# Where a step of the edge stage does its share of the next group's binning

## The reference

```python
xn = _layernorm(x, axis=-1)
x = x + _L0_gnn_ref(xn, edge_weight, src, dst) + _L0_mix_ref(xn[None], ...)[0]
x = x + _L0_ffn_ref(_layernorm(x, axis=-1)[None], ...)[0]
...
def _L0_gnn_ref(x, values, row, col):     # row = src, col = dst
    msgs = values[:, None] * x[col]
    return jax.ops.segment_sum(msgs, row, num_segments=N_NODES)
```

## Time and profile before

| | |
|---|---|
| median of 3 runs | 2460.25 us (2447.17 to 2464.95) |
| the profiled execution | 2457.84 us, span 2455.5 us, mean granted TensorE clock 0.938 |
| TensorE matmul busy | 2100.7 us (86%) |
| TensorE weight loads busy | 1796.0 us (73%) |
| VectorE / ScalarE / GpSimd busy | 1567.8 (64%) / 1074.1 (44%) / 1503.6 (61%) |
| gathers L1087 | 1029, mean 1186 ns |
| edge stage | from 339.2 us to about 1947 us of the span |

### The profile page before, as it was taken

One profiled execution on the slowest core, in us unless ns is written; L12 is line 12 of the kernel. 1 busy time (PEld: TensorE's weight loads), 2 busy tenths in 40 slices (PEclk: granted clock), 3 DMA queues, 4 the chain that ended last, 5 costly groups with the idle time before them and its releaser, 6 DMA issues. The chain is left out here.

```text
span 2455.5 us, 39205 instructions
## 1 busy us (share of the span) xinstructions
PE 2100.7 (86%) x11850; PEld 1796.0 (73%) x11851; DVE 1567.8 (64%) x2845; ACT 1074.1 (44%) x3171; POOL 1503.6 (61%) x1293
## 2 busy tenths in 40 slices
PE   4678668999899889989998999899999883888880
PEld 2356557888788778878887888788888783666660
DVE  6787558866786788578758875877444459233326
ACT  2331025556455545655555555555666420222220
POOL 1000268877777777688778877867777530676760
PEclk8898889999999999999999999999999856999995
DMA  5422372223222322233232223222333420566658
GB/s 194 161 81 71 109 234 77 85 86 95 78 82 86 93 76 83 85 89 86 85 88 85 84 87 91 78 85 84 91 101 101 120 99 0 167 186 181 186 163 313
DMA packets 157053, 271.50 MB, mean 111 GB/s; under 512 B 27730, under 2 KB 104513, under 8 KB 156770
## 3 DMA queue, kind: packets, MB, share of 16 engines
q0 software_dynamic: 59584, 161.78, 22.0%
q1 hardware_dynamic: 84534, 91.92, 12.1%
q10 hardware_dynamic: 12780, 15.84, 1.8%
HBM read 224.64 MB, written 45.76 MB: 110 GB/s over the span
## 5 line engine op out<-in xcount | busy, mean ns | idle before, releaser
L1087 POOL DMA_INDIRECT edge_G<-xn_scratch,edge_row_i x1029 | 1220.7, 1186 | 371.4 <-issue 272.5
L1148 ACT ACTIVATE edge_weighted<-edge_hots,bins_scale 128x128 f32<-128x128 bf16 x2401 | 738.4, 391 | 51.5 <-DVE edge_row_hots L1176 51.5
L1116 PE MATMUL edge_op<-edge_win,edge_A 128*128 128x256 f32 x2744 | 654.0, 381 | 0.0
L1116 PEld LDWEIGHTS edge_op<-edge_win,edge_A 128*128 128x128 f32 x2744 | 526.4, 192 | 73.2
L1112 PE MATMUL edge_op<-edge_G,edge_weighted 128*128 128x256 f32 x2058 | 513.2, 386 | 69.7 <-DMA edge_G<-xn_scratch,edge_row_i 57.1
L1139 ACT COPY edge_A<-edge_ap 128x512 f32<-128x512 f32 x343 | 200.9, 586 | 680.1 <-PE edge_ap L1103 680.1
L1112 PEld LDWEIGHTS edge_op<-edge_G,edge_weighted 128*128 128x128 f32 x2058 | 367.9, 192 | 117.4 <-issue 55.0
L1171 DVE TENSOR_TENSOR edge_hots<-bins_iota128b,bins_recb 128x1024 bf16<-128x1024 bf16 x343 | 236.6, 690 | 331.2 <-PE edge_ap L1103 324.2
L1103 PE MATMUL edge_ap<-edge_weighted,edge_row_hots 128*128 128x128 f32 x2744 | 363.3, 275 | 23.1 <-DMA edge_win<-xn_scratch 13.5
L1103 PEld LDWEIGHTS edge_ap<-edge_weighted,edge_row_hots 128*128 128x128 f32 x2744 | 341.7, 192 | 41.2 <-DMA edge_win<-xn_scratch 13.9
L1176 DVE TENSOR_TENSOR edge_row_hots<-all_iota,bins_recd 128x512 f32<-128x512 f32 x343 | 235.2, 686 | 0.0
(11 more groups left out here) (245 smaller groups left out, 1907.8 us busy)
## 6 DMA issues: line engine op xcount, KB each, us to landing
exp_w1x<-in_w SPq DMA_DIRECT2D x105, 256.0 KB
edge_G<-xn_scratch,edge_row_i POOLq DMA_INDIRECT x1029, 3.0
ln_xin<-in_x SPq DMA_DIRECT2D x12, 512.0 KB, 5.1
xn_scratch<-ln_xnb ACTq DMA_DIRECT2D x12, 512.0 KB, 5.7
xnT_scratch<-ln_xT SPq DMA_DIRECT2D x12, 512.0 KB, 6.8
mix_xg<-xn_scratch SPq DMA_DIRECT2D x12, 512.0 KB, 3.9
mix_ek<-xnT_scratch SPq DMA_DIRECT2D x12, 512.0 KB, 4.5
mix_xg<-in_x SPq DMA_DIRECT2D x12, 512.0 KB, 4.0
```

The source lines that it names most:

```text
L1087: pool.indirect_dma_start(out=G[:, row_buffer(b), i, :], out_offset=None, in_=xn_dram, in_offset=bass.IndirectOffsetOnAxis(ap=row_i[:, b * ...
L1116: last = nc.tensor.matmul(op[j][:, :], A[:, j, i, :], win[:, q % 2 * DN + i, :], start=False, stop=i == DN - 1)
L1148: last = nc.scalar.activation(weighted[:, buf, i, :], hots[:, b % 2, i // 2, :, i % 2], ACT.Copy, scale=scale[:, b, i:i + 1])
```

## The change

`pe_share` for step b is called inside `products`, between the A products and the waits for `summed` and for the gathered rows. Before, it was called behind `products`, so behind the window products that raise `stepped`. What remains behind `products` is the check of the last group's bounds at its step 0. No instruction is added or removed, and the order on the other engines is as it was.

```diff
@@ -1103,6 +1103,8 @@
                         last = nc.tensor.matmul(ap[j][:, i * P:(i + 1) * P], row_hots[:, j, i, :],
                                                 weighted[:, buf, GN + i, :], start=True, stop=True)
                     last.then_inc(a_done, 1)
+                    if q + 1 < NQ:
+                        bins.pe_share(pe, q + 1, b)
 
                     if t >= 2:
                         pe.wait_ge(summed, t - (0 if b == 0 else 1))
@@ -1121,9 +1123,7 @@
                     pe.wait_ge(win_in[q % 2], (q // 2 + 1) * 16 * DN)
                     for b in range(NB):
                         products(q, b)
-                        if q + 1 < NQ:
-                            bins.pe_share(pe, q + 1, b)
-                        elif b == 0:
+                        if q + 1 == NQ and b == 0:
                             pe.wait_ge(flag_in, 1)
                             nc.tensor.transpose(mm[0:1, 0:P], most1[:, :], ident[:, :])
                             nc.tensor.transpose(mm[0:1, P:P + NCH], bins.span[:, :], ident[0:NCH, 0:NCH]).then_inc(bounds, 1)
```

## The result

The kernel after takes 2439.81 us (median of 7 runs, 2438.05 to 2443.93), the kernel before 2455.25 us in runs beside it (7 runs, 2447.17 to 2464.95). The ratio is 0.9939 with a 95% interval of 0.9916 to 0.9961: 15 us less, a third of it forecast. The profiled executions differ by 17.3 us of span, 2455.5 to 2438.2.

The account below looks back on a forecast made before the run. TensorE, 86% busy, was taken to wait only in steps 1 to 16, bound by GpSimd's gathers. Hidden binning 4.0 plus clock 0.9 gave 4.9 us off the 2460.25 median: 2455, range 2438 to 2467.

Parts of the forecast that it names:

- the rival for which its low end was kept: The first rival: VectorE's head start shortens steps 9 to 15, 2443 us, 15%; its further reach widened the low end.
- part 2: Step 15 binning hidden in the wait for gathers, 1.0 us each in groups 0, 1, 2 and 5: 4.0 us saved.
- first stretches that move by 2 us or more: Sign of being wrong: steps 0 to 16 of the groups moving together by 2 us or more either way.
- Order in the wall: Steps 17 to 42, six groups: binning between A and gathered products leaves no hole and hides nothing, 0.
- Clock: After group 1's wait: binning within it keeps half of the 1.77 us lost to the lower TensorE clock, 0.9 us.
- Base sums on TensorE: Step 8: seven small matmuls, 0.47 us, ahead of the gathered products; nothing on the path, 0 (at most 2.8).
- VectorE's head start: Steps 9 to 13: VectorE's long work starts 2.0 us earlier, but the gather is late next, so 0 on the path.
- The first rival: VectorE's head start shortens steps 9 to 15: 17 us saved if all 2.0 us per group come through, 2443; 15%.
- The rival of worse collisions: The same head start hits worse gathers in the first stretches: 7.7 us slower, 2468; 13%.
- the fourth: It does nothing: gathers of steps 16 and 17 become late, the 1.0 us is waited out a step later; 2460, 15%.

Follow-up runs that it names:

- the kernel with the head start taken back: Kernel after, but VectorE waits at step 9 for step 8's window products before using the base sums: 2447.66 us, ratio 0.9957 to the kernel before.

## Why the prediction was right, and which step was off

The time was within the range and within 1%, and the sign was right. Its forecast was 4.9 us less; 15 came. That the time still fell into the range is owed to the rival for which its low end was kept, not to the parts that the forecast summed: of these, part 2 at most gave something, the 1.0 us of group 0. One of the prediction's own signs of being wrong, first stretches that move by 2 us or more, is there in groups 1, 2 and 5 (4.2, 5.7 and 3.9), though not in all together.

1. *Order in the wall, no cost:* right; 4.92 us per step, no hole between the kinds of matmul, 150.0 us per wall.
2. *Binning in the wait, 4.0 us:* right where that wait exists (about 1.0 us less of it in the profile with the binning alone, 6.0 us in the median), and nothing carried over into the wall. In the kernel after it saves almost nothing, since step 15 no longer waits except in group 0. (The half of group 1 was written 4.3 us before the wait by these rows, not 4.2; nothing hangs on it.)
3. *Clock, 0.9 us:* it did not come as put. In groups 1 to 5 the lower clock now follows the wait at step 12 (2.90 us for six gathered products at 866.26, 2.75 to 2.90 in all five), so the slow stretch moved and nothing was won. The rule cited from the Trainium skill (TensorE: Matmul & The Clock Gate, The HAM clock gate) agrees with that row too; it says nothing of where the wait will stand.
4. *Base sums on TensorE, 0:* right as a cost.
5. *VectorE's head start, 0:* this is the term that was mis-sized. Put at 0, it measured 13.5 us with the base sums alone. That these us come through VectorE is read from the traces: the pause at step 14 in 15 of 15 groups with the head start and in none of 20 without it, where slot operations and GpSimd's lead were the old ones. The times of the kernel with the head start taken back don't show it by themselves. Its argument, that GpSimd's chain is unbroken and so doesn't care about an earlier VectorE, overlooked that the length of the chain is itself made by VectorE: the gathers of steps 9 to 17 take 39.8 us in group 2 before and 34.9 after. The first rival had the mechanism and the price, 17 us less (2443), and was given 15%. What spoke for it was on the page: the earlier trace rows has groups of 82 and of 88 us with identical work, and two ways for one program to run ask what decides between them. Reading VectorE's lag step by step in groups 2 and 3 would have shown 3.1 and 1.7 us at step 14, and no pause in either.

The rival of worse collisions was wrong in sign on the first chips; the fourth, that step 16 takes the gain back, did not occur. The Trainium skill (SBUF — State Buffer, Who interferes with whom) calls the ports that VectorE shares with GpSimd an exclusive lock, which the first to issue has for its whole instruction. The gather of 3.55 us was held over three VectorE operations that follow each other, to the first that reads PSUM; here the measurement goes further than the rule. Its statement that a reduction does not contend agrees with the gather of 0.95 us at 865.76, wholly under L426 (865.48 to 867.46) in group 2 of the kernel after.

## What to carry to other kernels

When repeated groups with identical work differ in a profile, find what state they differ in before costing an edit; a shift of 2 us on an engine that is never the bound can decide it. In this kernel VectorE blocks GpSimd by working without a break more than by the amount of its work, so the catching up after a delay is the dear part, and one well-placed wait (0.012 of the ratio) was worth more than faster operations (nothing). A wait placed by a fixed step holds only if the engine is not too late for it, so look in the trace whether it does. And a gain explained on one chip may come another way on the next: there the same change brought 23 us with the step 15 waits in place.

## What the runs showed of the hardware

- Gathers of GpSimd take 0.95 us undisturbed, and up to 3.6 us when VectorE runs `tensor_tensor` operations on SBUF one behind the other; the long ones end 0.8 us after the end of a VectorE operation, most often of L1176, ahead of the addition that reads PSUM (163 of the 433 gathers over 1.05 us in the kernel before), but also between two operations on SBUF.
- The same program takes 2455 to 2459 us on the first chips and 2598 us on another, with "issue" gaps of up to 4.9 us on ScalarE and 4.4 us on TensorE's window products, and with "remote" waits of up to 7.5 us. The change's ratio differs as well, 0.9939 against 0.9895.
